# Another written-out order for the two streams of a ViT tower kernel

## The reference

```
h = tokens(x)                                   # patch product, class token, position
h = h + attention(layernorm(h))                 # one head of 192, softmax over 197 keys
h = h + expert_ffn(layernorm(h))                # one of 3 experts per image: the argmax of a softmax over the tokens' mean
h = h + attention12(layernorm(h))               # 12 heads of 16 features, then a projection
h = h + ffn_and_routed_cls(layernorm(h))        # 192 -> 768 -> 192 with gelu; the first 6 tokens go through routed atoms instead
```

## Time and profile before

| | |
|---|---|
| median of three runs | 3344.58 us |
| the profiled execution | 3345.71 us |
| its span, first to last instruction | 3343.9 us |
| mean granted clock of TensorE | 0.937 |
| TensorE busy, matmuls | 2851.5 us, 85% |
| VectorE busy | 2035.6 us, 61% |
| ScalarE busy | 1344.4 us, 40% |
| GpSimd busy | 358.9 us, 11% |
| moved by DMA | 287.54 MB, mean 86 GB/s |

### The profile page before, as it was taken

How to read it: one execution, slowest core, us unless ns; L and a number is a source line. 1 busy time by engine, 2 the same in 40 slices (tenths; PEclk the granted TensorE clock), 3 DMA queues, 4 the chain that set the end, 5 groups by cost and what they waited for, 6 DMA issues and landing times.

```text
span 3343.9 us, 64120 instructions
## 1 busy us (share of the span) xinstructions
PE 2851.5 (85%) x23190; PEld 2632.7 (79%) x23190; DVE 2035.6 (61%) x5286; ACT 1344.4 (40%) x2840; POOL 358.9 (11%) x746
## 2 busy tenths in 40 slices
PE   4688889888988898888888988888889888988748
PEld 3578788888887888788888887888888878888647
DVE  4356666666666666666666656656666666566524
ACT  2144444444443444444434444444344444444311
POOL 0101111011111110111111101111111011110000
PEclk9689999999999999999999999999999999999868
DMA  5234333443343334433433344334333443333330
GB/s 152 77 64 102 84 76 84 101 99 71 89 100 85 76 84 101 99 71 89 99 86 75 85 101 99 70 90 100 85 74 86 101 99 70 90 86 85 61 89 4
DMA packets 127222, 287.54 MB, mean 86 GB/s; under 512 B 28790, under 2 KB 95367, under 8 KB 116172
## 3 DMA queue, kind: packets, MB, share of 16 engines
q1 hardware_dynamic: 127180, 286.97, 38.4%
HBM read 192.23 MB, written 15.00 MB: 62 GB/s over the span
## 4 chain that ended last, share of the span: by engine, by line
PE 58%; DVE 20%; DMA 8%; SPq 6%; issue 5%; ACT 3%; DVEq 0%; POOL 0%; ACTq 0%; POOLq 0%
PE banks L641 29%; PE banks L689 15%; DMA shared<-low 7%; PE banks L796 6%; DVE inv L1073 4%; DVE hx L968 3%; PE banks L814 3%; DVE stats L954 2%; PE banks L665 1%; SPq L501 1%; SPq L502 1%; SPq L506 1%; DVE sums L1071 1%; DVE xnT L994 1%; PE banks L827 1%
## 5 line engine op out<-in xcount | busy, mean ns | idle before, releaser
L1062 DVE TENSOR_REDUCE nmax<-banks 99x4 f32<-99x788 f32 x384 | 363.8, 976 | 165.7 <-PE banks L796 162.5
L796 PE MATMUL banks<-shared,q_stack 128*99 128x198 f32 x1536 | 231.8, 293 | 143.8 <-DMA shared<-low 103.5
L1238 ACT ACTIVATE probs_rest<-banks 99x396 f32<-99x396 f32 x512 | 242.8, 501 | 269.3 <-PE banks L814 264.6
L585 POOL TENSOR_TENSOR var_eps<-moments,eps 99x2 f32<-99x2 f32 x256 | 49.8, 194 | 2785.0 <-DVE moments L959 2785.0
L796 PEld LDWEIGHTS banks<-shared,q_stack 128*99 128x99 f32 x1536 | 192.2, 193 | 165.3 <-issue 117.1
L814 PE MATMUL banks<-q_stack,shared 128*99 128x198 f32 x1536 | 294.1, 288 | 21.6 <-ACT probs_rest L1238 13.1
L641 PE MATMUL banks<-tok_wT,xT 128*99 128x192 f32 x1536 | 276.1, 331 | 0.9 <-ACT xT L1194 0.9
L641 PE MATMUL banks<-tokT,fc_wT 128*128 128x198 f32 x1920 | 272.3, 297 | 1.3 <-DVE tokT L994 1.3
L1073 DVE RECIPROCAL inv<-sums 128x198 f32<-128x198 f32 x192 | 267.2, 1392 | 6.6
L689 PE MATMUL banks<-w_sb,hidT 128*99 128x192 f32 x1536 | 265.7, 326 | 0.0
L689 PE MATMUL banks<-fc_wT,hidT 128*99 128x192 f32 x1536 | 265.7, 326 | 0.0
(11 more groups left out here) (190 smaller groups left out, 5502.7 us busy)
## 6 DMA issues: line engine op xcount, KB each, us to landing
shared<-w_split SPq DMA_DIRECT2D x64, 1188.0 KB
xin<-in_x_dram SPq DMA_DIRECT2D x32, 1176.0 KB
w_sb<-in_L_ffn_W_dram SPq DMA_DIRECT2D x64, 576.0 KB, 7.8
w_last<-w_split SPq DMA_DIRECT2D x64, 384.0 KB
q_stack<-hi SPq DMA_DIRECT2D x128, 148.5 KB
q_stack<-low SPq DMA_DIRECT2D x128, 148.5 KB
shared<-hi SPq DMA_DIRECT2D x128, 148.5 KB
shared<-low SPq DMA_DIRECT2D x128, 148.5 KB
```

The costliest lines, as they stand in the source:

```text
L585: g.tensor_tensor(var_eps[p][:], moments[p][:, :, 1], eps[0:R, 0:T], ALU.add).then_inc(eps_added[p], 1)
L796: last = t_.matmul(b[n % 4][0:R, t * SP_:(t + 1) * SP_], q_stack[p][:, n, t * R:(t + 1) * R], k_stack[p][:, n, :], start=True, stop=True)
L1062: v.tensor_reduce(nmax1[p][:, :, 2 * j:2 * j + 2].rearrange("p t h -> p h t"), src, AX, ALU.max, negate=True).then_inc(nmax1_ready[p], 1)
L1238: s_.activation(ring(p, s).rearrange("p k s -> p (k s)"), b[s % 2][0:R, 0:T * SP_], ACT.Exp).then_inc(p1_ready[p], 1)
```

## The change

The list of stages and the merge string are replaced. The stages themselves, `AHEAD`, `B_FIRST`, all waits and all other functions stay.

```diff
-FLOW = ("""hid0_0 hid0_1 hid0_2 out0_0 out0_1 stat3 x norm3 turn3 tok0 tok1 stat1 qk1_0 norm1 qk1_1 v1 turn1 v0 q0 max0
-        max1 max2 max3 max4 max5 maxT s0 att0 p0 att1 att2 o0 att3 stat2 att4 att5 att6 norm2 att7 att8 att9 att10
-        turn2 att11 att12 att13 route proj stat4 load norm4 turn4 hid1_0 hid1_1 hid1_2 out1_0 out1_1""")
+FLOW = ("""hid0_0 hid0_1 hid0_2 out0_0 out0_1 x stat3 norm3 tok0 turn3 tok1 stat1 norm1 qk1_0 qk1_1 turn1 v1 q0 v0 max0
+        max1 max2 max3 max4 max5 maxT s0 p0 att0 att1 o0 stat2 att2 norm2 att3 att4 att5 att6 att7 att8 att9 att10
+        att11 att12 att13 turn2 proj stat4 route load norm4 turn4 hid1_0 hid1_1 hid1_2 out1_0 out1_1""")
...
-MERGE = ("baabababaaabrabbbbaabbbbaababbaaabbbbraarbrabaabbaabbbababbaabbaababaabaaaaabrrr"
-         "aabaaaababababbababbabaabbabbabababbaabbb")
+MERGE = ("abbaaabbabaabbabbabbbbaababraaabbrraabbbbaabraabababababrbbbaabbababaaaabaabaaba"
+         "bbaaabaaabaabbabaabababbrabbarbababbaabbb")
```

## The result

The changed kernel takes 3376.48 us (median of four runs, 3375.09 to 3383.18) against 3344.95 us; the ratio is 1.0095, with a 95% interval of 1.0083 to 1.0107. That is slower by more than the 0.2% that a measurement tells apart. The forecast of 3316 us had the wrong direction. The profiled execution took 3383.18 us, with a span of 3381.3 us, 37.4 us more than before; its mean granted clock is 0.925, where it was 0.937. At 1.2 GHz half of the clock is granted, so TensorE ran (1 - 0.925) x 2 x 3381 = 507 us at that level, before (1 - 0.937) x 2 x 3344 = 421 us.

What follows compares the result with a forecast made beforehand. TensorE was taken as the bound (busy 85%), with copies setting the stretches from `qk1_0` to `max0`. Terms -1.25 - 1.1 + 0.2 + 0 + 1.7 - 0.5 = -0.95 us, -29 over 31 periods: 3316 us, range 3260 to 3385.

Steps and rivals of the forecast that it cites:

- A's copies: A's stretch from `qk1_0` to `max0`, set by eight copies: ends at 14.9 instead of 14.73 us, +0.2 (0 to 1.2).
- B's copies: B's stretch from `qk1_0` to `max0`: the queue still holds copies, so nothing of VectorE's delay arrives, 0 (0 to 1.2).
- attention stretch: From `att0A` to `qk1_0B`: exponentials lie beside `o0` and `tok`, `turn2A` leaves; 1.25 us a period saved (0.34 to 1.6).
- `p0B` to `qk1_0A`: `x` ahead of `stat3` saves 1.1 us waiting, `att13B` adds 0.81, `turn2B` takes off 0.34, exponentials 0.46: -1.1 a period.
- clock behind A's maxima: A's work ends before its copies land, so its maxima start at the low clock: +1.7 us a period (0 to 2.4).
- clock in B: B's last hole before its maxima shrinks from 3.2 to about 2.2 us, giving 0.5 us a period back (0 to 1.3).
- rival 3: Nothing comes of it: waits for exponentials only change places (0.6 lost), B's clock stays low (0.5); +0.15, 3350 us; chance 0.13.
- waits for exponentials: Between `p0B` and `qk1_0A`, about 0.46 us of them go, since `hid0_0A` and `o0B` follow `att1B` at once.
- late third copy: In A's copy stretch SP sends its third copy 1.0 us late, and 0.6 us of the delay arrives at the landing.
- Rival 1: Slower: the late `low` is paid in full, both streams' copies land 1.2 us later; +1.75 a period, about 3400 us; chance 0.23.
- Rival 2: Faster: A's low clock falls inside its wait and costs nothing; -2.65 us a period, 3263 us; chance 0.16.
- two signs: The forecast is wrong if A's copies land beyond 15.5 us or if A's maxima start at full clock.

Runs made afterwards that it cites:

- after_fill_28_6: The changed kernel with matmuls that nobody reads ahead of the first score maxima's wait, 28 in A and 6 in B: 3301.06 us.
- after_fillA: The changed kernel with 28 matmuls that nobody reads ahead of A's first score maxima, none in B: 3314.43 us.
- before_fillB: The kernel before, in the old order, with 28 matmuls that nobody reads ahead of B's first score maxima, none in A: 3383.80 us.
- before_x: The kernel before, in the old order, with one edit of the new one, `x` ahead of `stat3` in the list: 3403.41 us.
- before_fill3: The kernel before, in the old order, with unread matmuls ahead of `v0` (17 in A, 10 in B) and `max0` (6 and 28): 3320.30 us.
- after_fillAB: The changed kernel with matmuls that nobody reads ahead of the first score maxima of both streams, 28 in A and 20 in B: 3261.11 us.

## Why the prediction was wrong, point by point

| step | predicted, us a period | measured |
|---|---|---|
| A's copies | +0.2 | +0.1 |
| B's copies | 0 | 0 |
| attention stretch, at full clock | -1.25 | -0.6 |
| `p0B` to `qk1_0A` | -1.1 | -0.84 |
| clock behind A's maxima | +1.7 | +2.0 |
| clock in B | -0.5 | +0.76, of which -0.19 order and +0.95 clock |
| sum | -0.95 | +1.4 |

Measured is what the profiles of the kernels before and after show. By the medians the sum is +1.0; which step holds the 0.4 less isn't shown.

The step that failed is the clock in B: "In B the last hole gets shorter (about 2.2 instead of 3.2), and I take 0.5 back". This term had the wrong sign. The hole did get shorter, to 2.32, and the clock cost more: over the full-clock floors of 12.89 (old order) and 12.70 (new) B lost 1.07 us a period before and 2.02 after. The premise, a price that goes with the wait, was wrong in a single period, as after_fill_28_6 shows, and in the kernel before every one of the 26 periods paid 0.9 to 1.3 us (13.79 to 14.19 us), while in the kernel after 22 of them took 14.4 us or more. Why they did is open. Whether the wait in A takes part in it isn't shown either: in the profile of after_fillA B's mean is 14.17 with nothing changed in B, but that was the fastest of four executions, and by the medians after_fillA gains 62 us, which is A's 2.01 us in 31 periods and nothing more.

The clock behind A's maxima was right in kind and 0.3 too small. All that the clock changed came to +2.6 (4.10 - 1.52; the two terms came to +3.0, and 0.4 that the old order paid under A's copies went) instead of +1.2, and with the order's terms as forecast that alone would have brought the change from -0.95 to +0.4, from faster to slower.

The attention stretch was mis-sized: 30.36 us before and 29.76 in after_fillA, both at full clock, so 0.6 instead of 1.25. That is about what rival 3 took off (0.6). Windows from A's first attention step to `qk1_0B`, first of the kernel before, then of the one after, and TensorE of the kernel after in `o0` and in an attention step, answers to the earlier trace rows:

```profile
1623.23:1635.32 12.09, 11.37 (x102) 9.67 (x101) 10.77 (x33) 6.05 (x13) 3.44 (x7) 1.00 0.00 0
```

```profile
1644.62:1656.09 11.47, 10.52 (x98) 9.17 (x97) 9.85 (x34) 4.96 (x11) 1.95 (x5) 1.00 0.00 0
```

```profile
1646.04 1.54 PE L641 MATMUL banks<-vals,turned 99*99 99x192 f32 x8 [0.55 <-DVE turned L1013]
...
1654.48 0.43 PE L814 MATMUL banks<-q_stack,shared 128*99 128x198 f32 x2 [0.41 <-ACT probs_first L1238]
```

It takes 11.47 us where 10.84 was forecast. TensorE's busy time fell by 0.85, about the 0.34 and 0.5 of the forecast, but its idle time rose from 0.72 to 0.95: a hole of 0.41 for an exponential is still there, and `o0` now waits 0.55 for the turned weights. The forecast had that wait "as today", but the kernel before has no such wait at its `o0`.

`p0B` to `qk1_0A` gave 0.84 of 1.1. The wait in `x` went as forecast (0.38, near 0.4), and TensorE's busy time grew by 0.41, close to the 0.47 of the two moved stages. What failed is the 0.46 of waits for exponentials: beside the 1.56 in `x` TensorE was idle there for only 0.16 us, so they weren't there to be saved.

A's copies came out right for a wrong reason. I read the 0.5 us between A's 14.74 and B's 14.26 as `q0`'s place on VectorE. At full clock the old order has 14.3 (before_fillB, before_x, before_fill3), so 0.4 us of it was the low clock under the copies, which I had taken as free. The late third copy then cost 0.5, close to the 0.6 worked out from the queue, and the two cancel. Rival 1 is refuted: both streams' copies end as before, and what was slow came after them. Rival 2, that A's low clock costs nothing, is refuted for the kernel as it stands. The kernel nearest to it is after_fillA, with A's price gone, and that takes 3314 us. That after_fillAB's 3261 is so close to the rival's 3263 is luck: there all of B's price is gone, where the rival took 0.5 off, and the order itself gains less than the rival had it.

Neither of the two signs by which the forecast was to be found wrong came: A's copies landed in time, and A's maxima start at the low clock. It named no sign for the clock in B, where it failed. That 3376 us lie inside the wide range of 3260 to 3385 is no credit to it either: that end of the range stood for rival 1. Two small readings were off without effect: by its own terms and the earlier trace rows the work under the copies ends 3.5 (A) and 4.5 us (B) short of them, not "some 6", and eight copies of 148.5 KB are 1.22 MB, which take 9.9 us at 123 GB/s, not 9.7.

## What to carry to other kernels

Where a wait of TensorE comes round in every pass, ask not only how long it is but what stands right behind it: in A 3.55 us of idle time, most of it earlier under the copies, cost 0.4 us, and a wait of 3.02 us directly ahead of a full stretch of matmuls 2. Cost an order at a steady clock and the clock apart, with unread matmuls in the wait as the probe, because the low clock moves when one wait is cured and its prices don't add. If the probe pays, as here (2.45% below the kernel before), it can stay as a part of the kernel, sized to the wait and measured again after every change of the order.

## What the runs showed that I had not expected

The low clock isn't a fixed price of a wait: 1.59 us of wait ahead of the same matmuls cost 2.70 us in one period and 0.0 in another of one execution, and 28 matmuls in B's wait of the old order made the kernel 1.3% slower; in its trace the low clock has moved into A's maxima and, in some periods, behind `p0B`. And the low clock can cost under a wait, too: A's copy stretch of the old order took 14.74 us with a granted clock of 0.88 and 14.31 with 1.00.
